# Expert routing in four parts behind the batches, with token lists written to DRAM by indirect writes

## What is computed

```python
x = x + layernorm(attn(layernorm(x)))      # q, k, v with bias; ctx = (q k^T) v without softmax,
                                           # group norm over each of 32 heads, output projection
x = x + layernorm(ffn(layernorm(x)))

# ffn, T = 4096 tokens, E = 8 experts, inner width 704
shared = (silu(xf @ sg.T) * (xf @ su.T)) @ sd.T
probs = softmax(xf @ gate_w.T)
topw, topi = top_k(probs, 2);  topw = topw / (topw.sum() + 1e-20)
comb = zeros(T, E).at[arange(T), topi].add(topw)
routed = sum_e ffn_e(xf) * comb[:, e]
out = shared + routed
```

## Time and profile before

| | us |
|---|---|
| median of 3 runs (855.82 to 856.79) | 856.46 |
| the profiled execution | 857.45 |
| its span, first to last instruction | 855.7 |

### The profile page before, as it was taken

The page is one execution under the profiler, slowest core; times in us unless marked ns, Lnnn a source line. Parts: engine busy times, 40 slices in busy tenths (PEclk is TensorE's granted clock), DMA queues, the critical chain, the costliest instruction groups (busy, mean ns, idle before and its releaser), DMA issues.

```text
span 855.7 us, 21069 instructions
## 1 busy us (share of the span) xinstructions
PE 786.6 (92%) x6583; PEld 643.3 (75%) x6592; DVE 586.6 (69%) x1591; ACT 484.8 (57%) x1068; POOL 291.6 (34%) x316
## 2 busy tenths in 40 slices
PE   6889999999999998666899999999999999999991
PEld 2447777777777776544788888888888888888880
DVE  6668889898988888894887444555555555555553
ACT  2264848485757675422566555565656565656562
POOL 3011010101010100062265555555555555555542
PEclk9999999999999999997999999999999999999996
DMA  4104334443535252502245545646463646464733
GB/s 191 50 25 179 112 142 112 152 125 144 145 121 152 101 156 74 148 1 71 50 68 77 100 76 73 123 76 145 72 148 70 148 69 148 68 146 68 147 42 96
DMA packets 102691, 90.10 MB, mean 105 GB/s; under 512 B 63760, under 2 KB 94224, under 8 KB 101456
## 3 DMA queue, kind: packets, MB, share of 16 engines
q1 hardware_dynamic: 87648, 68.45, 27.7%
q0 software_dynamic: 14976, 20.78, 16.0%
HBM read 48.70 MB, written 27.39 MB: 89 GB/s over the span
## 4 chain that ended last, share of the span: by engine, by line
PE 68%; DVE 17%; ACT 6%; issue 4%; DMA 3%; POOL 1%; ACTq 0%; SPq 0%; DVEq 0%; POOLq 0%
PE ps L911 39%; PE ps L926 18%; PE ps L991 3%; DVE wgu L1286 3%; PE ps L1023 3%; DVE hf L1226 2%; ACT wgu L771 2%; PE ps L985 2%; DVE wdn L1286 1%; DVE st L1402 1%; DVE st L1206 1%; DVE wdn L1535 1%; PE ps L952 1%; DVE hT L1236 1%; ACT silu L723 1%
## 5 line engine op out<-in xcount | busy, mean ns | idle before, releaser
L911 PE MATMUL ps<-xhl,wgu 128*128 128x256 f16 x3102 | 386.3, 274 | 13.1 <-DMA xhl<-attw 6.5
L911 PEld LDWEIGHTS ps<-xhl,wgu 128*128 (+1 forms) x3102 | 302.9, 98 | 57.6 <-issue 10.4
L1226 DVE SCALAR_TENSOR_TENSOR hf<-ps,sc,silu 128x256 f32<-128x256 f32 x330 | 159.6, 484 | 187.5 <-ACT silu L723 148.2
L926 PE MATMUL ps<-wdn,hT 128*128 (+1 forms) x1870 | 253.7, 274 | 11.3 <-DVE hT L1236 8.9
L723 ACT ACTIVATE silu<-ps,sc 128x256 f32<-128x256 f32 x275 | 130.4, 474 | 234.1 <-PE ps L911 211.4
L926 PEld LDWEIGHTS ps<-wdn,hT 128*128 128x128 f16 x1870 | 182.4, 98 | 37.1 <-DVE hT L1236 6.3
L672 POOL DMA_INDIRECT acc_d<-ysb,gst x78 | 129.2, 1657 | 44.5 <-POOL gst L668 30.9
L605 POOL TENSOR_TENSOR rstd<-ve,mhalf 128x4 f32<-128x4 f32 (+1 forms) x32 | 30.7, 960 | 297.5 <-DVE ve L1211 276.2
L1236 DVE TENSOR_TENSOR hT<-hf,hT 128x256 f16<-128x256 f32 x275 | 115.1, 418 | 1.7
L737 ACT CAST hT<-hf 128x256 f16<-128x256 f32 x275 | 109.8, 399 | 10.2 <-DVE hf L1226 8.4
L661 POOL DMA_INDIRECT attw<-xn_d,gst x78 | 80.4, 1031 | 44.5 <-POOL gst L657 32.6
(11 more groups left out here) (241 smaller groups left out, 775.2 us busy)
## 6 DMA issues: line engine op xcount, KB each, us to landing
wgu<-in_gu SPq DMA_DIRECT2D x8, 1408.0 KB, 6.0
att<-in_x SPq DMA_DIRECT2D x16, 512.0 KB, 5.5
wdn<-in_dn SPq DMA_DIRECT2D x8, 768.0 KB, 8.1
x_d<-att SPq DMA_DIRECT2D x8, 512.0 KB, 2.9
xn_d<-wgu SPq DMA_DIRECT2D x8, 512.0 KB, 3.3
acc_d<-ysb SPq DMA_DIRECT2D x16, 256.0 KB, 3.1
att<-x_d SPq DMA_DIRECT2D x8, 512.0 KB
att<-acc_d SPq DMA_DIRECT2D x7, 512.0 KB
```

The source lines that it names most:

```text
L911: ins = te.matmul(o, slot_gu(slot, hw, k, j), x(hx, k), start=(n == 0), stop=(n == len(TERMS) - 1))
L926: ins = te.matmul(y_bank(u, tt), h(hh), slot_dn(slot, c, hw), start=(c == 0 and n == 0 and tt == 0), stop=(c == FC - 1 and n == 1 and tt = ...
L1226: v.scalar_tensor_tensor(out=hf[lo:P, c % 2 * TW:(c % 2 + 1) * TW], in0=up, scalar=scale_of(slot, 1, lo, P), in1=silu[lo:P, c % 2 * TW:(c ...
```

## The change

The routing has four parts, batches 0 to 2, 3 and 4, 5 and 6, and 7 (`PART_B`). Part 0 is handled in batches 3 and 4, part 1 in batches 5 and 6 (`EXTRA`), part 2 in the last batch, part 3 in the tail. The steps are finer: `route_norm` is split from `route_top1`, `route_weights` from `route_top2`. The matmul step `route_slots` of a part gives ranks over all earlier tokens with bf16 operands (a strict upper triangle, ones over earlier batches' sums and over earlier tiles), in the free half of the PSUM bank `max_ps`. Every expert has its own range of 4096 slots (`expert_at`), so that a token's slot is known without the later counts.

For parts 0 to 2 the token numbers are written by GpSimd, one indirect DMA for each tile and each of the two choices, 56 in all, 128 single words each, into `ids_d` in DRAM, which SP has filled with zeros at the start. GpSimd issues them behind roots, in the numbers that `EXTRA` and `LAST_ORDER` give. Three semaphores go round, so that a column waits for the one three before it. Only part 3 uses one-hots: one group for 16 columns (the first tile of each expert) in the tail, and the other 62 in routed tiles 2 and 3 (`LATE`). Two matmuls add the lists read back from DRAM: `ids_first` by SP in the tail, `ids_rest` by an indirect gather on GpSimd with the expert order as key. Each part's combine weights are stored by SP separately. The waits for `eid_made` move to routed tile 8, which is the first that needs the order.

```diff
+PART_B = ((0, 3), (3, 5), (5, 7), (7, 8))
+EXTRA = {3: {("H", 1): [("route_probs", 0)], ("H", 3): [("route_norm", 0)], ("H", 6): [("route_top1", 0)]},
+         4: {("H", 1): [("route_top2", 0), ("route_slots", 0)], ("H", 3): [("route_positions", 0)], ("H", 6): [("route_weights", 0)],
+             ("ctx_norm",): scatters(0, 0, 1), ("lno_stats",): scatters(0, 1, 3), ("x2",): scatters(0, 3, 6)},
+         5: {("H", 1): [("route_probs", 1)], ("H", 3): [("route_norm", 1)], ("H", 6): [("route_top1", 1)],
+             ("ln1_stats",): scatters(0, 6, 7), ("ctx_norm",): scatters(0, 7, 8), ("lno_stats",): scatters(0, 8, 10), ("x2",): scatters(0, 10, 12)},
+         6: {("H", 1): [("route_top2", 1), ("route_slots", 1)], ("H", 3): [("route_positions", 1)], ("H", 6): [("route_weights", 1)],
+             ("ctx_norm",): scatters(1, 0, 1), ("lno_stats",): scatters(1, 1, 4), ("x2",): scatters(1, 4, 8)}}
+LAST_ORDER = [("ctx",), ("G", 0), ("ctx_out",), ("G", 1), ("channel_stats",), ("H", 0), ("group_mean",), ("H", 1), ("route_probs", 2), ("G", 2),
+         ("group_var",), ("G", 3), ("H", 2), ("route_norm", 2), ("G", 4), ("ctx_norm",), ("H", 3), ("H", 4), ("out",), ("route_top1", 2), ("G", 5),
+         ("lno_stats",), ("D", 0), ("G", 6), ("route_top2", 2), ("route_slots", 2), ("H", 5), ("G", 7), ("D", 1), ("D", 2), ("lno_apply",),
+         ("route_positions", 2)] + scatters(2, 0, 3) + [("G", 8), ("D", 3), ("H", 6), ("x2",)] + scatters(2, 3, 8) + [
+         ("H", 7), ("D", 4), ("H", 8), ("D", 5), ("ln2_apply",), ("route_weights", 2), ("H", 9), ("D", 6), ("G", 9), ("D", 7),
...
+TAIL = [("G", 0), ("route_norm", 3), ("H", 0), ("G", 1), ("route_top1", 3), ("G", 2), ("H", 1), ("D", 0), ("route_top2", 3), ("G", 3), ("H", 2),
+        ("route_slots", 3), ("D", 1), ("route_weights", 3), ("G", 4), ("H", 3), ("D", 2), ("route_positions", 3), ("one_hots", 0), ("G", 5),
+        ("invert", 0), ("route_indices", 0), ("H", 4), ("D", 3), ("G", 6), ("H", 5), ("D", 4), ("route_counts",), ("route_segments",), ("G", 7), ("H", 6),
+        ("D", 5), ("route_order",), ("G", 8), ("H", 7), ("D", 6), ("route_table",), ("G", 9), ("H", 8), ("D", 7), ("G", 10), ("H", 9), ("D", 8),
+        ("G", 11), ("H", 10), ("D", 9), ("H", 11), ("D", 10), ("D", 11)]
...
+LATE |= {(2, 2): ("one_hots", 0, 1), (2, 4): ("invert", 0, 1), (3, 0): ("indices", 0, 1)}
...
+            sp.wait_ge(zeros_made, 1)
+            for h in range(2):
+                sp.dma_start(ids_rows[h * P:(h + 1) * P, :], logits[:, :]).then_inc(ids_cleared, 16)
...
+            store_comb(2)
+            for r in range(RINGS):
+                sp.wait_ge(ids_scattered[r], 16 * 2 * len(range(r, PART[LAST][0], RINGS)))
+            sp.wait_ge(m_made, LAST + 1)
+            sp.dma_start(ids_first, ids_d.rearrange("(e c) o -> e (c o)", c=TOK)[0:E, 0:TW]).then_inc(first_loaded, 16)
+            store_comb(LAST)
...
+            def scatter_ids(n, j):
+
+                pool.wait_ge(pos_made, n + 1)
+                if j == 0:
+                    pool.wait_ge(ids_cleared, 32)
+                wait(pool, ids_scattered[j % RINGS], 16 * 2 * (j // RINGS))
+                for m in range(2):
+                    g.indirect_dma_start(ids_d, bass.IndirectOffsetOnAxis(ap=posi[:, m * NTB + j:m * NTB + j + 1], axis=0), tokf[:, j:j + 1], None).then_inc(ids_scattered[j % RINGS], 16)
...
+            def ranks(n):
+
+                t0, t1 = PART[n]
+                pe.wait_ge(const_made, 9)
+                pe.wait_ge(m_made, n + 1)
+                pe.wait_ge(max_read, spreads[0])
+                dst = rank_bank(n)
+                te.matmul(dst, upper16[:, :], m16[:, E * t0:E * t1], start=True, stop=False)
+                for b in range(PART_B[n][0]):
+                    te.matmul(dst.rearrange("p (t e) -> p t e", e=E), ones16[:, :], each(bsum16[:, E * b:E * b + E], t1 - t0), start=False, stop=False)
+                for t in range(t0, t1 - 1):
+                    ins = te.matmul(dst[:, E * (t + 1 - t0):].rearrange("p (t e) -> p t e", e=E), ones16[:, :], each(m16[:, E * t:E * t + E], t1 - 1 - t),
+                                    start=False, stop=(t == t1 - 2))
...
+            def invert(n):
+
+                pe.wait_ge(onehot_made, n + 1)
+                pe.wait_ge(onehot_lo_made, POOL_H + 1)
...
+                    pe.wait_ge(first_loaded, 16)
...
+                for h in range(TT):
+                    te.matmul(dst.rearrange("p (i h) -> p i h", h=TT)[:, :, h], rows[:, h * P:(h + 1) * P], cols, start=(h == 0), stop=False)
+                for h in range(OHB):
+                    for m in range(2):
+                        ins = te.matmul(dst, oh_lo[:, m, h, :], oh_hi[n][:, m, h, :], start=False, stop=(h == OHB - 1 and m == 1))
...
+                if kind == "route_norm":
                     dve.wait_ge(exp_made, n + 1)
                     rl(v.tensor_reduce(ms, te8(pr), AX.X, ALU.add))
                     rl(v.reciprocal(mr, ms))
                     rl(v.tensor_tensor(te8(pr), te8(pr), by_tile(mr), ALU.mult))
...
+                    dve.wait_ge(ranked, n + 1)
+                    at = expert_at[:, :].rearrange("p (o e) -> p o e", o=1).to_broadcast([P, count, E])
+                    v.tensor_tensor(te8(xx), te8(rank_bank(n)), at, ALU.add).then_inc(rank_read, 1)
+                    dve.wait_ge(rank_read, n + 1)
+                    v.tensor_tensor(cc, o1, xx, ALU.mult)
+                    rl(v.tensor_tensor(pr, o2, xx, ALU.mult))
+                    v.tensor_reduce(posf[:, t0:t1], te8(cc), AX.X, ALU.add)
+                    rl(v.tensor_reduce(posf[:, NTB + t0:NTB + t1], te8(pr), AX.X, ALU.add))
...
```

More of the change, by code:

```diff
@@ new lines, in order_of @@
+def order_of(b):
+    steps = []
+    for step in ORDER:
+        if b < NPRE or not step[0].startswith("prep"):
+            steps += [step] + EXTRA.get(b, {}).get(step, [])
+    return steps
+LAST_ORDER = [("ctx",), ("G", 0), ("ctx_out",), ("G", 1), ("channel_stats",), ("H", 0), ("group_mean",), ("H", 1), ("route_probs", 2), ("G", 2),
[3 more added lines that the diff above has]
+         ("H", 7), ("D", 4), ("H", 8), ("D", 5), ("ln2_apply",), ("route_weights", 2), ("H", 9), ("D", 6), ("G", 9), ("D", 7),
+         ("turn2",), ("G", 10), ("xhl",), ("H", 10), ("rows2",), ("G", 11), ("D", 8), ("logits",), ("D", 9), ("logits_out",), ("D", 10),
+         ("H", 11), ("route_probs", 3), ("D", 11)]
@@ L110 @@
 PROGRAM = [(step[0], step[1:]) for step in START]
-PROGRAM += [(b, step) for b in range(1, B - 1) for step in ORDER if b < NPRE or not step[0].startswith("prep")]
+PROGRAM += [(b, step) for b in range(1, B - 1) for step in order_of(b)]
 PROGRAM += [(B - 1, step) for step in LAST_ORDER]
@@ L204, in build @@
         last_gu, last_dn = att[:, 0:KD * GU], att[:, KD * GU:KD * GU + FC * D]
[L207 to L211, removed]
+        routes = wdn[:, (E - 1) * SLOT_DN:E * SLOT_DN].bitcast(F32)
+        r_p, r_t, r_o1, r_o2, r_c, r_x = (routes[:, NTB * E * n:NTB * E * (n + 1)] for n in range(6))
+        route_rest = spare[:, 2 * KD * S + 2 * NT * D:SLOT_GU].bitcast(F32)
@@ L219, in build @@
[L219 to L226, removed]
+        OHB, POOL_H = NT, 1
@@ L317, in build @@
         counted = sem("counted")
+        ranked = sem("ranked")
+        rank_read = sem("rank_read")
+        pos_made = sem("pos_made")
+        zeros_made = sem("zeros_made")
+        ids_cleared = sem("ids_cleared")
+        ids_scattered = [sem(f"ids_scattered{n}") for n in range(RINGS)]
+        keys_made = sem("keys_made")
+        first_loaded = sem("first_loaded")
+        rest_loaded = sem("rest_loaded")
         eid_made = sem("eid_made")
@@ L1026, in _ @@
                         ins.then_inc(att_done, 1)
+                if kind == "route_slots":
+                    ranks(step[1])
                 if kind == "turn2" and b in PE_SECOND:
@@ L1044, in _ @@
                 if kind == "route_slots":
-                    pe.wait_ge(m_made, 2)
-                    x2_ready(pe, B - 1)
-                    te.matmul(att_ps[0][:, 0:256], upper[:, :], r_m, start=True, stop=True)
-                    te.matmul(att_ps[0][:, 256:512], ones[:, :], r_m, start=True, stop=True).then_inc(counted, 1)
+                    ranks(step[1])
+                if kind == "route_counts":
+                    pe.wait_ge(logits_made, B)
+                    for b in range(B):
+                        ins = te.matmul(att_ps[3][:, E * b:B * E].rearrange("p (t e) -> p t e", e=E), ones16[:, :], each(bsum16[:, E * b:E * b + E], B - b),
+                                        start=(b == 0), stop=(b == B - 1))
+                    ins.then_inc(counted, 1)
                 if kind == "route_order":
@@ L1053, in _ @@
                 if kind == "invert":
[L1055 to L1064 removed]
+                    invert(step[1])
             def routed(i, r, slot, before, later=None):
@@ L1302, in by_tile @@
                 return a.rearrange("p (t o) -> p t o", o=1).to_broadcast([P, a.shape[-1], E])
```

(11 more changed lines are left out.)

239 lines of the change are left out of this document (143 added, 96 removed), and 4 rows, old and new, of the table LAST_ORDER.

## The result

The changed kernel took 926.33 us (median of four, 925.15 to 926.79), the kernel before 856.19 beside it: a ratio of 1.0816, 95% interval 1.0798 to 1.0835. Forecast were 858.3, at most 865.5. The profiled execution took 925.15, 923.4 of it span, where 855.7 was before: 67.7 us to be found.

A forecast was written before the change was run, and what follows sets the result against it. TensorE was taken to bound batches 2 to 6, VectorE the tail. Batches +14.5, tail -15.7 (last batch included), routed tiles +1.3 and clock +1.7 gave +1.8: 859.3 profiled, 858.3 us predicted, range 848.5 to 865.5.

The forecast's parts named there:

- The paragraph on GpSimd: Batches 4 to 6 and last: 56 indirect writes at 1.3 us each, at most 1.9, delaying the reciprocal roots queued behind.
- Clock: Half-clock matmuls after TensorE gaps of 2 us in batches 4 and 6: +1.7 us, from 0 to 3.4.
- Batches 3 to 6: Added routing steps meet almost no VectorE slack and stop TensorE: 2.2, 5.1, 2.5 and 4.7, together +14.5 us, GpSimd included.
- the rival by which the batches have room: Batches 3 to 6: VectorE's idle time takes in half or more of the new steps; -8.5, 849.8 us; chance 0.25.
- GpSimd's roots: Reciprocal roots queued behind writes: two columns fit between, three miss by 0.9; 0.7 us in batch 5, 0.4 in batch 6.
- The rival built on it: Batches 4 to 6 and last: a write costs 1.9 us on GpSimd and holds the roots; +7, 865 us; chance 0.15.
- The first list is late: Tail: list load waits for writes, inversion for the load; past 387 the gap before routed tiles stays, +6; chance 0.03.
- Last batch and tail: Last batch slips +2.2 us; tail loses VectorE work, routed tiles start 14.1 earlier and run 1.6 faster: -15.7 in sum.
- Routed tiles: Tiles 2 and 3 take the other columns' inversion (0.7) and indices (0.6): +1.3 us, from 0.7 to 2.5.

The follow-up runs named there:

- steps moved: The changed kernel without its indirect writes, with norm, top1 and weights of batches 3 to 6 moved behind lno_apply: 855.40 us, ratio 0.9976 to the kernel before.
- both remedies: The whole changed kernel with list words spread within their 256 places and routing steps of batches 3 to 6 moved behind lno_apply: 863.84 us, ratio 1.0087.
- whole rows: The changed kernel, each indirect write storing 128 rows of 512 bytes to another tensor in place of words, lists left zero: 863.8 us.
- lists permuted: The whole changed kernel with place 16b + a made 16a + b within each 256 places, neighbours 64 bytes apart: 868.73 us, ratio 1.0140.

## Why the prediction was wrong

**The step that failed: the writes.** The paragraph on GpSimd took the indirect writes for their 1.3 us each on the issuing engine, between a gather and an accumulating scatter, and asked only who is queued behind them there. That was measured right: 0.96 of issue and 0.30 behind it, as the gather's. But an indirect DMA has two prices, and for the second, from issue to landing and what that does to others' transfers, the forecast had no term and no range; no row of before showed a one-word write to DRAM. Comparing the change with its kernel without writes, stage by stage: 16.9 us in batch 4, 15.0 in batch 5, 10.1 in batch 6, 20.2 in the last batch and the tail, 1.5 ahead of batch 1 and 0.6 in the routed tiles. The six pauses above are 54.3 us, 2.33 of which the kernel without writes has as well, so about 52 of the 64; another 9 lie in TensorE's own busy time, 44.93, 43.29 and 44.22 in the three batches against 41.36, 41.04 and 41.19, at clocks of 0.89, 0.88 and 0.91 against 1.00, parts of them at half clock.

**Clock.** 1.7 us were taken for it in pauses of 2 us, from 0 to 3.4. Those pauses (forecast for batches 4 and 6) came, 2.21 and 2.00 us. Without writes they are 2.22 and 1.93 and cost nothing: the clock stays at 1.00 there. That is luck in part, for with the steps moved the same pause of 1.93 in batch 6 is followed by a stretch of half clock. The next twelve matmuls of G, without writes and then with the steps moved:

```profile
288.82 1.47 PE L1001 MATMUL ps<-wgu 128*128 128x256 f16 x12
```
```profile
285.40 2.66 PE L1001 MATMUL ps<-wgu 128*128 128x256 f16 x12
```

In the tail without writes the clock does fall, 0.87. The 9 us of the kernel after lie in stages with pauses of 7 to 12 us that were not foreseen.

**Batches 3 to 6: right.** Without the writes their steps cost 2.6, 5.9, 1.7 and 4.6 (43.58, 46.83, 43.31 and 45.52 against 40.95, 40.95, 41.64 and 40.95), 14.8 together; forecast were 2.2, 5.1, 1.8 and 4.3 without GpSimd's share, 13.4. Reading VectorE's slack as zero at those places was right, and the rival by which the batches have room fell. Most of what is missing is in batch 4: up to the projection it loses 4.2 us (12.4 from its group mean against 8.3), behind it 1.7, where 4.0 and 1.1 were forecast. The weights take 1.7 there (213.77 to 215.48), so the 0.55 us of slack that was taken off them was not there. TensorE's pause before the ranks is as foreseen:

```profile
199.47 0.20 PE L1057 MATMUL ps<-wgu 128*128 128x96 bf16 x1 [2.21 <-issue]
```

What the forecast did not see is that this price hangs on the place. The gap of 2.00 us before the residual add was written off because the step after H6 lies ahead of it; steps put right behind lno_apply do fall into it, and 4.9 us come back in these four stages, 6.4 between the medians of the whole.

**GpSimd's roots: mechanism right, small.** In batch 4, with two columns between them, the two roots lie 8.14 us apart, 8.10 without writes: nothing, as forecast. In batch 6, with three, they lie 9.46 apart in place of 8.00, the second straight behind a write: 1.5 us, where a miss of 0.9 was forecast and 0.4 priced. With the words 512 bytes apart, where the same issues stand and the stores land in 2.9, batches 4, 5 and 6 take 46.86, 43.71 and 47.73 us, 0.0, 0.4 and 2.2 more than without writes; 1.6 of the last is TensorE's busy time, at a clock of 0.96. Forecast for GpSimd were 0, 0.7 and 0.4.

```profile
345.37 1.22 POOL L700 DMA_INDIRECT ids_d<-tokf,posi  x1 [0.30 <-issue]
346.60 1.04 POOL L680 TENSOR_TENSOR rstd<-ve,mhalf 128x4 f32<-128x4 f32 x1
```

The rival built on it had the sign but neither place nor size of the loss: GpSimd waits for its writes here (34.6 us), and the issue of a write was not the longer one that this rival wanted.

**The first list is late: named, and mis-sized.** It had 0.03, and 6 us, on the ground that the writes end near 353 and only their issue counts. In the run, the last write is issued at 426.38 and takes 16.15, so it ends at 442.5, and the load behind it lets the inversion start at 444.13, after a pause of 12.78 us that is 2.33 without writes. The mechanism should have been priced by landing time, not by issue time.

```profile
426.38 16.15 DMA ids_d<-tokf,posi
```

**Last batch and tail: gain there, smaller.** Without writes the last batch slips by 3.2 (forecast 2.2), and the tail takes 40.10 us where 37.9 was forecast; VectorE's busy time in it, 23.24, is the 23.2 of the sum. The missing 2 us are pauses, two of which the sum lacked or had too short: 2.33 at the inversion (0.8 forecast) and 3.00 before L1186, a matmul on the tile order that VectorE makes one step ahead. Behind the second, and behind the first with one of 2.31 that follows it, twelve matmuls take about 2.5 to 2.8 us (kernel without writes):

```profile
380.40 0.58 PE L1071 MATMUL ps<-ident,wgu 8*128 8x8 f32 x4 [2.33 <-issue]
...
384.83 2.77 PE L1001 MATMUL ps<-wgu 128*128 128x256 f16 x12
...
394.62 0.45 PE L1186 MATMUL ps<-upper,ones 128*128 128x78 f32 x2 [3.00 <-DVE upper L1686]
394.90 2.47 PE L1001 MATMUL ps<-wgu 128*128 128x256 f16 x12
```

From batch 7's group mean to the first routed tile the gain is then 11.0, not 14.1. In the kernel after, that gain is there too, under 20 us of waiting. And the routed tiles start as foreseen, with no pause and at full clock, 4.12 us for 36 matmuls where 5.57 was the earlier trace rows:

```profile
469.82 4.12 PE L1008 MATMUL ps<-xhl,wgu 128*128 128x256 f16 x36
```

**Routed tiles: right.** From there to the end it is 453.0 us without writes and 453.4 before: -0.4, forecast -0.3 (-1.6 and +1.3).

So all terms but one sum to +4.4, where +1.8 was forecast, and that one is 64 to 66 us. Left open: why the first 69 us take 1.5 us more in some kernels (the change, with reads, 16 bytes apart in either kernel, steps moved, both remedies) and not in others (no writes, 8, 64 and 512 bytes apart, whole rows, lists permuted), with edits that don't touch them; and how much of the 8 us for spaced writes is GpSimd's time, how much small descriptors and how much the permutation.

## What to carry to other kernels

Price an indirect DMA twice: the issue on its engine, and the landing, with everything that waits for any transfer landing beside it. A scatter of single words into adjacent places of DRAM is to be avoided or spaced by at least 16 bytes; the permutation that spaced them by 64 took four small operations a part; and where a trace of before has no such write, the range must say so, or a probe of the write alone must come first. An extra step costs what the place leaves: behind the operation that another engine is about to answer it was nearly free, in front of one that TensorE waits for it cost its full length.

## What the runs showed of the hardware that was not expected

- 56 indirect writes of 128 adjacent 4-byte words cost 44 us in a kernel that they have nothing to do with, 28 KB in all; 9 with the words 16 bytes apart. Their median landing was 8.7 and 3.4 us, and as reads in the changed kernel they cost 5 (one timing); of the 9 and the 5, 1.5 each lie ahead of batch 1.
- They delay transfers of other queues: a 512 KB store issued by SyncE took 15.7 us to land, where the median before was 2.9, and the last shared expert's weights 14.8 and 18.2 us in place of 5.9 and 7.7, from the lists of DMAs of after and before:

```profile
att<-in_gu SPq DMA_DIRECT2D x1, 1408.0 KB, 14.8
...
att<-in_dn SPq DMA_DIRECT2D x1, 768.0 KB, 18.2
```
```profile
att<-in_gu SPq DMA_DIRECT2D x1, 1408.0 KB, 5.9
...
att<-in_dn SPq DMA_DIRECT2D x1, 768.0 KB, 7.7
```

- In the kernel without writes pauses of TensorE of 2.22 and 1.93 us in a busy batch left its clock at 1.00, and pauses of 2.3 and 3.0 us in the tail were followed by twelve matmuls in 2.5 to 2.8 us in place of 1.5. With the steps moved, the same pause of 1.93 us in batch 6 was followed by twelve in 2.66: here the length of one pause does not tell whether the clock falls.
